# A fused two-layer gated cross-attention kernel: where ScalarE's evictions, the copy of the column sums, the normalising of x and the tail's second scores stand in the order of work

## The chip, the cores and the metric

The kernel runs on one core of one Trainium2 chip. The metric is the device time of one execution in microseconds (us), lower is better. Engines are called by their names and, in rows, by the letters of the profile: PE is TensorE (PEld its weight loads), DVE is VectorE, ACT is ScalarE, POOL is GpSimd, SP is the engine that issues DMAs here.

## The reference, cut to what matters

Batch 8, 512 tokens, width 256, 16 heads of 16, in float32. `x` and `ctx` are (8, 512, 256).

```
x = x + tanh(g_xattn[0]) * L0_xattn(layernorm(x), ctx)     # pruned softmax attention
x = x + tanh(g_ffn[0])   * L0_ffn(layernorm(x))            # fp4-rounded SwiGLU, inner width 704
x = x + tanh(g_xattn[1]) * L1_xattn(ctx, layernorm(x))     # linear attention, layer norm
x = x + tanh(g_ffn[1])   * L1_ffn(layernorm(x))            # int8-rounded linear

def L0_xattn(q, kv):                     # after the projections, per batch and head
    p    = softmax(q @ k.T / 4)          # 512 x 512
    idx  = top_k(p.sum(over queries), 460)
    p    = p * mask(idx)                 # 52 key columns are dropped, no renormalising
    return concat(p @ v) @ Wo.T + bo
```

The column sums of `p` decide which keys are dropped, so the kernel computes the scores twice: once to get row maxima, row sums and column sums, and once, much later, to make the final `p` that multiplies `v`.

## The kernel before, in words

**Units and steps.** The attention is cut into 16 units (8 batches x 2 groups of 8 heads). A unit has 16 steps; one step `z` handles two heads (h = 0, 1) and one block of 128 tokens. So the attention has 256 steps (`ALL_Z`) and a tail of 48 more (`LAST = ALL_Z + LAG + 6`, `LAG = 42`), in which only the second half of the work is left. Each engine has its own program, a loop over `z`, and the engines meet only by semaphores.

**What a step does on each engine.** TensorE at step z: two *first scores* into half of `ps_a` (L1253, it waits for the first exponentials of step z-2), two *second scores* of step z-43 into `ps_b` (it waits for the second exponentials of step z-44), two column sums into `ps_s` (L1289), two products with `v` (L1303, rows 64 to 127 of the same bank `ps_s`), and then, in most steps, a piece of a *fill*. VectorE: row maxima `nmax` (L1329) of the first scores, reciprocals (L1340), one step of the selection of the dropped keys (`rank_step`), one step of the shifts. ScalarE: the two *first exponentials* `ea` (L1428), and the *second exponentials* `prob` of step z-42 (L1444, one instruction of 1024 columns; from step 256 on two of 512 columns with a semaphore each, L1441).

**The selection.** Once per unit, at step 16u+20, VectorE copies the column sums out of `ps_s` into `rank` (`rank_step(u, 0)`, L1372). TensorE's column sums of the next unit go to the same rows and wait for that copy (`s_rank`). Seven rounds of MAX8 and MATCH_REPLACE8 follow, one instruction a step.

**Fills.** The projections of the following batches, 16 pieces of work a batch (XT0, XT1: transposes of x; CT0, CT1: of ctx; Q0, Q1, K0, K1: projections; V0, V1; GRAM; and X1, RB, KV, MM, ROW: products for the second layer), are put into the steps by a formula (`turn_of`: 0.7 pieces a step from step 41 on). TensorE issues a piece at the end of its step. Up to step 40 fills take turns in three PSUM banks; from step 41 on they have one, `ps_f`, and a fill waits until the one before it has left. A fill is moved out of PSUM by ScalarE (XT, CT, Q, K, GRAM, MM) or VectorE (the others). ScalarE does this at the end of its own step z, behind `prob`: up to step 41 for fills that end in TensorE's step z, and from step 41 on for those that end in TensorE's step z+1 (function `leaving`).

**Normalising x.** The layer norm of batch b+1 before its projections is four instructions of 128x256 in place in `x_in` (`normal`, L1011), two in ScalarE's fill GRAM of batch b and two in its fill ROW. TensorE's transposes XT0 and XT1 of batch b+1 read them. GpSimd's own in-order work there is: splitting q and k into two float16 halves (L748, L750), three small parts of a row (L738 to L742), and once a unit copying `v` into a padded tile (`pad`, L1240), which waits for TensorE.

**The tail.** From step 256 (n = z - 256) on TensorE has the last second scores and products with `v`, and beside them the first two units of the feed-forward layer: `first_product` at n = 6, 12 and 28, a transpose at 17 and 30, and `gate_or_up` (L1712, into two halves of `ps_a` in turn, moved out by ScalarE at L1887) at n = 19 to 26 and 32 to 39. In ScalarE's step the second exponentials come first, and then, where there is one, the eviction L1887.

```
            b = within(z - LAG - 1, ALL_Z)      # TensorE, step z
            if b is not None:
                second(b)
```

Of the kernel before, what the change touches and what calls it, by code (L numbers as in the profile page):

```python
# [206 lines left out]
def prepare(m, a, w, ey, tiles, bank):  # L207
# [6 lines left out]
    s_gate, s_turned = m.sem("gate"), m.sem("w_turned")  # L214
    s_w8q, s_w8t, s_bcol = m.sem("w8_rounded"), m.sem("w8_turned"), m.sem("bias_turned")
    names = {WQ: "L0_xattn_Wq", WK: "L0_xattn_Wk", WV: "L0_xattn_Wv", WO: "L0_xattn_Wo", WK1: "L1_xattn_Wk",
# [62 lines left out]
    def tensor(e):  # L279
# [13 lines left out]
        def bias_columns():  # L293
            e.wait_ge(ey.s_bias, 1)
            for n in range(2):
                for c in range(DC):
                    ins = e.transpose(bank[3][:, n * DC + c:n * DC + c + 1],
                                      brow2[:, n, c * P:c * P + P], w.ident[0:1, 0:1])
            ins.then_inc(s_bcol, 1)

# [14 lines left out]
    def scalar(e):  # L315
# [4 lines left out]
        def leave(n):  # L320
            k = TURNS.index(n)
            e.wait_ge(s_turned, k + 1)
            if n == WO:
# [12 lines left out]
        def done():  # L336

            e.wait_ge(s_turned, 6)
            e.wait_ge(s_w8t, 1)
            e.wait_ge(s_bcol, 1)  # L340

        return gate, leave, done

    def vector(e):
# [10 lines left out]
        def bias_columns():  # L355
            e.wait_ge(s_bcol, 1)
            e.tensor_scalar(ey.cols[:, 0], bank[3][:, 0:DC], 0.25, None, ALU.mult)
            e.tensor_copy(ey.cols[:, 1], bank[3][:, DC:2 * DC]).then_inc(ey.s_bias, 1)
# [215 lines left out]
def project(m, a, w, ey, scr, bank, fp4):  # L574
# [11 lines left out]
    for n in range(FILLS, FILLS * B + ROW + 1):  # L586
# [24 lines left out]
        m.sem(f"dve_{n}") for n in ("x1", "rb", "kv", "mean", "row", "c1w"))  # L611
    s_act_m, s_act_gram, s_pool_r = m.sem("act_m"), m.sem("act_gram"), m.sem("pool_r")

# [115 lines left out]
    def gpsimd(e):  # L729
# [14 lines left out]
        def halves(dst, x, c, b, stored, done):  # L744
# [5 lines left out]
            e.tensor_tensor(dst[:, 1, c], x, dst[:, 0, c], ALU.subtract).then_inc(done, 1)  # L750

        def fill(s):
            n = SEQ[s]
            if n < 0 or not real(n):
                return
            b, k = n // FILLS, n % FILLS
            if n in QK:
                e.wait_ge(s_act_full, QK.index(n) + 1)
# [10 lines left out]
    def tensor(e):  # L769
# [5 lines left out]
        def fill(s, part):  # L775
# [62 lines left out]
            elif k in (XT0, XT1):  # L838
                e.wait_ge(s_act_xn, b + 1)
                transposes(dst, ey.x_in[p], k - XT0).then_inc(s_pe_xT, 1)  # L840
# [158 lines left out]
    def scalar(e):  # L999
# [24 lines left out]
        def fill(s):  # L1024
# [48 lines left out]
            elif 0 < b < B - 1:  # L1073
                if k == Q0:
                    guess(b + 1)
                elif k in (GRAM, ROW):
                    normal(b + 1, int(k == ROW))

# [14 lines left out]
def attend(m, w, scr, tiles, fp4):  # L1093
# [156 lines left out]
    def tensor(e):  # L1250
# [55 lines left out]
        def step(z):  # L1306
            if z < ALL_Z:
                first(z)
            b = within(z - LAG - 1, ALL_Z)
            if b is not None:  # L1310
                second(b)
            g = within((z - 4) // 2, ALL_G)
# [8 lines left out]
    def vector(e):  # L1321
# [76 lines left out]
        def step(z):  # L1398
            if (z - LAG - 12) % (2 * TT) == 0:
                n = within((z - LAG - 12) // (2 * TT), 2 * UNITS)  # L1400
                if n is not None:
                    leave(n)
            if z < ALL_Z:
                maxima(z)
            if z % 2:
                g = within((z - 3) // 2, ALL_G)
                if g is not None:
                    reciprocals(g)
            u, n = (z - HALVES - 4) // HALVES, (z - HALVES - 4) % HALVES
            if 0 <= u < UNITS and n < 2 * ROUNDS + 2:  # L1410
                rank_step(u, n)
# [6 lines left out]
    def scalar(e):  # L1418
# [27 lines left out]
        def step(z):  # L1446
# [4 lines left out]
            if z < ALL_Z:  # L1451
                first(2 * z)
                first(2 * z + 1)
            b = within(z - LAG, ALL_Z)
            if b is not None:
                second(b)

        return step

# [784 lines left out]
def run(nc, whole, w, pr, fp4, pj, at, fd):  # L2244
# [5 lines left out]
    with ExitStack() as ctx:  # L2250
# [5 lines left out]

        def leaving(z):

            return [*(ended(z) if z <= pj.open else ()), *(ended(z + 1) if z >= pj.open else ())]

        @block.sync
# [114 lines left out]
        def _(e):  # L2376
            (gate, leave_weight, prepared), fill = pr.scalar(e), pj.scalar(e)
            gate()
            step = at.scalar(e)

# [26 lines left out]
            for z in range(at.last):  # L2407
                step(z)
                for s in leaving(z):
                    fill_and_magnitude(s)  # L2410
                n = z - tail
                if n == 11:
# [137 lines left out]
```

## Time and profile before

| | us |
|---|---|
| median of 3 runs | 1252.24 (1250.3 to 1255.97) |
| profiled execution: its own time | 1255.39 |
| its span, first to last instruction | 1253.7 |
| steps 0 to 40 (44.5 to 170.2) | 125.7 |
| steps 41 to 255 (170.2 to 756.4) | 586.2 |
| tail, to the last product with `v` (756.4 to 863.6) | 107.2 |
| the feed-forward and second layer (863.6 to the end) | 390.1 |

A row of the profile gives an engine, a line of the kernel, what is written and read, how many, and the times; idle time stands with the engine and line that ended it. Times in the rows are us from the start of the span, unless marked ns. The stretches of the table are bounded by starts of L1428 and the end of the last L1303.

### The profile page before, as it was taken

To read this page: it belongs to the slowest core of one execution; us is meant where nothing else is said; L and a number is where in the kernel's file an instruction comes from. 1 tells how busy PE (TensorE), PEld (TensorE's weight loads), DVE (VectorE), ACT (ScalarE), POOL (GpSimd) and SP (SyncE) were. 2 spreads that over 40 slices of the span, in tenths; PEclk is the share of its full clock that TensorE was granted. 3 is DMA by queue.
4 is the path that set the end of the run, shared out by engine and by line. 5 is a ranking of instruction groups with operands and counts; after the bars stand their busy time and mean duration, and the time that the engine had idled before them with its cause. 6 is when DMAs were issued, how large, how long until landed. Compare 5 with 4: busy or idle time off the path is not lost.

```text
span 1253.7 us, 18028 instructions
## 1 busy us (share of the span) xinstructions
PE 1102.6 (88%) x5672; PEld 493.0 (39%) x5672; DVE 1004.8 (80%) x1977; ACT 944.4 (75%) x2135; POOL 236.0 (19%) x281
## 2 busy tenths in 40 slices
PE   7898898889898888889987879888999999999974
PEld 5433332222222222222321112224667677777652
DVE  7888877787787887787889886355899999999965
ACT  5566678889888898898979996465666776766744
POOL 5433320010011011101010101101222222222212
PEclk9999998999899999999989999989999999999986
DMA  9603141232123122213202211001011111110001
GB/s 289 167 34 88 58 110 31 48 93 55 50 68 71 52 58 66 60 30 94 46 25 51 44 50 41 18 5 42 27 51 43 35 59 43 35 60 26 18 17 34
DMA packets 75986, 71.79 MB, mean 57 GB/s; under 512 B 11834, under 2 KB 69492, under 8 KB 75892
## 3 DMA queue, kind: packets, MB, share of 16 engines
q1 hardware_dynamic: 75892, 70.64, 20.8%
q8 instruction: 46, 0.75, 0.2%
q14 instruction: 48, 0.39, 0.1%
HBM read 42.83 MB, written 27.28 MB: 56 GB/s over the span
## 4 chain that ended last, share of the span: by engine, by line
PE 58%; ACT 18%; DVE 14%; issue 7%; SPq 1%; POOL 1%; DMA 1%; DVEq 0%; ACTq 0%; POOLq 0%
PE ps_s L1289 12%; PE ps_a L1712 11%; ACT ea L1428 8%; PE ps_b L1670 6%; ACT prob L1444 6%; PE ps_b L1253 4%; DVE nmax L1329 3%; PE ps_s L1303 3%; PE ps_a L1253 3%; PE ps_s L1670 2%; PE ps_f L805 2%; PE ps_f L1685 2%; PE ps_f L834 2%; PE ps_a L1721 2%; PE ps_f L1746 1%
## 5 line engine op out<-in xcount | busy, mean ns | idle before, releaser
L1428 ACT ACTIVATE ea<-ps_a,nmax 128x512 f32<-128x512 f32 x512 | 356.2, 723 | 50.4 <-DVE nmax L1329 50.0
L1329 DVE TENSOR_REDUCE nmax<-ps_a 128x2 f32<-128x1024 f32 x256 | 312.5, 1221 | 98.9 <-PE ps_a L1253 97.4
L1289 PE MATMUL ps_s<-ea,rz 128*32 128x512 f32 x1024 | 283.1, 632 | 32.4 <-DVE rank L1372 30.1
L1303 PE MATMUL ps_s<-prob,v_pad 128*32 128x512 f32 x1024 | 282.3, 632 | 2.8 <-DVE att L1396 2.4
L1444 ACT ACTIVATE prob<-ps_b 128x1024 f32<-128x1024 f32 x214 | 228.3, 1067 | 21.8 <-PE ps_b L1253 21.2
L1712 PE MATMUL ps_a<-wgu,xT 128*128 128x352 f32 x512 | 166.2, 465 | 11.8 <-ACT ea L1887 9.2
L1253 PE MATMUL ps_b<-q_st,k_st 52*128 52x512 f16 x512 | 106.3, 395 | 42.4 <-ACT prob L1444 39.2
L1428 ACT ACTIVATION_READ_ACCUMULATOR ea<-ps_a,nmax 128x1 f32 x512 | 123.5, 241 | 0.0
L1253 PE MATMUL ps_a<-k_st,q_st 48*128 48x512 f16 x512 | 102.3, 395 | 20.5 <-ACT ea L1428 19.3
L1712 PEld LDWEIGHTS ps_a<-wgu,xT 128*128 128x128 f32 x512 | 92.8, 191 | 68.4 <-issue 24.3
L1887 ACT ACTIVATE ea<-ps_a 128x352 f32<-128x352 f32 x128 | 59.7, 467 | 58.0 <-PE ps_a L1712 57.5
L1670 PE MATMUL ps_b<-wdn,hT 128*128 128x256 f32 (+1 forms) x384 | 94.9, 392 | 0.0
L1253 PEld LDWEIGHTS ps_a<-k_st,q_st 48*128 48x128 f16 x512 | 24.9, 93 | 174.9 <-ACT ea L1428 100.7
L1289 PEld LDWEIGHTS ps_s<-ea,rz 128*32 128x32 f32 x1024 | 38.0, 109 | 117.2 <-issue 112.9
L1441 ACT ACTIVATE prob<-ps_b 128x512 f32<-128x512 f32 x84 | 45.7, 596 | 43.6 <-PE ps_b L1253 43.4
L1670 PEld LDWEIGHTS ps_b<-wdn,hT 128*128 128x128 f32 (+1 forms) x384 | 67.6, 189 | 22.5 <-issue 15.9
L1383 DVE MATCH_REPLACE8 rank<-top,rank 64x512 f32<-64x512 f32 x112 | 74.9, 668 | 0.1
L1377 DVE MAX8 top<-rank 64x8 f32<-64x512 f32 x112 | 73.5, 657 | 0.1
L1253 PEld LDWEIGHTS ps_b<-q_st,k_st 52*128 52x128 f16 x512 | 26.5, 94 | 102.6 <-ACT prob L1444 62.4
L2114 DVE SCALAR_TENSOR_TENSOR ea<-ea 128x512 f32<-128x512 f32 (+1 forms) x32 | 36.0, 1126 | 18.4 <-ACT ea L1866 10.3
L1303 PEld LDWEIGHTS ps_s<-prob,v_pad 128*32 128x32 f32 x1024 | 38.4, 109 | 25.8 <-issue 24.6
L1613 POOL TENSOR_TENSOR x_in<-x_in,rows 128x512 f32<-128x512 f32 x16 | 20.4, 1274 | 127.5 <-DVE r L2051 105.6
(276 smaller groups left out, 1773.1 us busy)
## 6 DMA issues: line engine op xcount, KB each, us to landing
k_scr<-k_p SPq DMA_DIRECT2D x24, 256.0 KB, 2.5
q_scr<-q_p SPq DMA_DIRECT2D x24, 256.0 KB, 2.9
q_st<-q_scr SPq DMA_DIRECT2D x32, 192.0 KB, 4.7
k_st<-k_scr SPq DMA_DIRECT2D x32, 192.0 KB, 5.0
c_in<-in_ctx SPq DMA_DIRECT2D x8, 512.0 KB, 4.2
x_in<-in_x SPq DMA_DIRECT2D x8, 512.0 KB, 5.2
v_scr<-v_s SPq DMA_DIRECT2D x8, 512.0 KB, 4.2
v_in<-v_scr SPq DMA_DIRECT2D x16, 256.0 KB, 3.2
```

What stands on the lines that cost most here:

```text
L1253: return e.matmul(bank, left[b][o:o + rows, r, t * P:t * P + P], right[b][o:o + rows, r], start=True, stop=True)
L1289: e.matmul(ps_s[32 * h:32 * h + 32, :], rz[:, t, r, 2 * k + h, o:o + 32], ea[g % RING][:, 2 * k + h], start=(n == 0 and k == 0), stop=(n = ...
L1303: e.matmul(ps_s[o:o + 32, :], v_pad[u % 2][:, t, 4 * r + 2 * k + h], at.prob[g % PROBS][:, 2 * k + h], start=(t == 0 and k == 0), stop=(t ...
L1329: e.tensor_reduce(nmax[u % 2][:, t].rearrange("p (h r) -> p r h", h=2)[:, r], ps_a[:, z % 2 * 2:z % 2 * 2 + 2], AX_X, ALU.max, negate=True ...
L1377: e.max(top[:, :], rank[:, :]).then_inc(*dv.up())
L1383: e.match_replace(rank[:, :], top[:, :], rank[:, :], NEG).then_inc(*dv.up())
L1428: e.activation(ea[c % RING][:, g % 4], ps_a[:, g % 4], ACT.Exp, bias=nmax[u % 2][:, t, n:n + 1], accum_out=tot[u % 2][:, t, n:n + 1]).then ...
L1441: e.activation(dst[:, h], ps_b[:, h], ACT.Exp).then_inc(done, 1)
L1444: e.activation(dst, ps_b[:, :, :], ACT.Exp).then_inc(s_prob, 1)
L1670: ins = e.matmul(dst[t], left(c, t), right(c), start=(first and c == chunks[0]), stop=(last and (apart or t == N - 1) and c == chunks[-1]))
L1712: ins = e.matmul(gu[:, q % 2, 0:HALF_F], xT[:, c, t * P:t * P + P], w.wgu[:, c, k * HALF_F:(k + 1) * HALF_F], start=(c == 0), stop=(c == D ...
L1887: e.activation(dst[:, t, k % 2 * HALF_F:(k % 2 + 1) * HALF_F], gu[:, q % 2, 0:HALF_F], func).then_inc(s_act_gu, 1)
```

## The change

Five edits. (1) ScalarE: the second exponentials become a function of their own (`later`), and fills that end in TensorE's step z leave in ScalarE's step z, between the first and the second exponentials. (2) VectorE: `rank_step(u, 0)`, the copy of the column sums, stands ahead of the step's maxima. (3) `normal` of batches 2 to 7 moves from ScalarE to GpSimd, at the same two fills; the transposes of these batches wait for a new semaphore of GpSimd. (4) TensorE, from step 256 on: second scores of step z-42 (at step 256 those of z-43 too). (5) One semaphore of the preparation is merged into another, which leaves its waits where they were.

```diff
@@ TensorE's fill: XT0, XT1
-                e.wait_ge(s_act_xn, b + 1)
+                if b < 2:
+                    e.wait_ge(s_act_xn, b + 1)
+                else:
+                    e.wait_ge(s_pool_xn, b - 1)
@@ GpSimd's fill
+        def normal(b, half):
+            p = b % 2
+            e.wait_ge(s_dve_nb, b + 1)
+            for t in (2 * half, 2 * half + 1):
+                ins = e.tensor_scalar(ey.x_in[p][:, t], ey.x_in[p][:, t], rs[p][:, t:t + 1], nb[p][:, t:t + 1],
+                                      ALU.mult, ALU.add)
+            if half:
+                ins.then_inc(s_pool_xn, 1)
...
+            if 0 < b < B - 1 and k in (GRAM, ROW):
+                normal(b + 1, int(k == ROW))
@@ ScalarE's fill
-                elif k in (GRAM, ROW):
-                    normal(b + 1, int(k == ROW))
@@ TensorE's step
-            b = within(z - LAG - 1, ALL_Z)
-            if b is not None:
-                second(b)
+            if z <= ALL_Z:
+                b = within(z - LAG - 1, ALL_Z)
+                if b is not None:
+                    second(b)
+            if z >= ALL_Z:
+                b = within(z - LAG, ALL_Z)
+                if b is not None:
+                    second(b)
@@ VectorE's step
+            u, n = (z - HALVES - 4) // HALVES, (z - HALVES - 4) % HALVES
+            if 0 <= u < UNITS and n == 0:
+                rank_step(u, n)
             if z < ALL_Z:
                 maxima(z)
...
-            if 0 <= u < UNITS and n < 2 * ROUNDS + 2:
+            if 0 <= u < UNITS and 0 < n < 2 * ROUNDS + 2:
                 rank_step(u, n)
@@ ScalarE's step and loop
             if z < ALL_Z:
                 first(2 * z)
                 first(2 * z + 1)
+
+        def later(z):
             b = within(z - LAG, ALL_Z)
...
                 step(z)
-                for s in leaving(z):
+                for s in ended(z):
                     fill_and_magnitude(s)
+                later(z)
```

ScalarE, steps around the evictions of two projections, with `ea` the first exponentials, `prob` the second and `full` the eviction of a fill. Before:

```order
L1428 ACTIVATE ea,tot0<-ps_a,nmax0 128x512 x2
L1444 ACTIVATE prob1<-ps_b 128x1024
L1022 ACTIVATE full1<-ps_f,cols 128x512
L1428 ACTIVATE ea,tot0<-ps_a,nmax0 128x512 x2
L1444 ACTIVATE prob1<-ps_b 128x1024
```

and after:

```order
L1446 ACTIVATE ea,tot0<-ps_a,nmax0 128x512 x2
L1035 ACTIVATE full1<-ps_f,cols 128x512
L1462 ACTIVATE prob1<-ps_b 128x1024
L1446 ACTIVATE ea,tot0<-ps_a,nmax0 128x512 x2
L1462 ACTIVATE prob2<-ps_b 128x1024
```

The eviction `full1` stands one pair of first exponentials later in ScalarE's program, and the second exponentials that were ahead of it are behind it.

VectorE, the step in which the column sums are copied (`rank<-ps_s`). Before:

```order
L881 BN_STATS st0<-x_in0 128x6 x2
L1329 TENSOR_REDUCE nmax0<-ps_a 128x2
L1372 TENSOR_SCALAR rank<-ps_s 64x512
L1363 STREAM_TRANSPOSE row1<-part 128x128
L1329 TENSOR_REDUCE nmax0<-ps_a 128x2
```

and after:

```order
L894 BN_STATS st0<-x_in0 128x6 x2
L1388 TENSOR_SCALAR rank<-ps_s 64x512
L1345 TENSOR_REDUCE nmax0<-ps_a 128x2
L1379 STREAM_TRANSPOSE row1<-part 128x128
L1345 TENSOR_REDUCE nmax0<-ps_a 128x2
```

One row of maxima and the copy changed places; nothing else on this engine moves.

TensorE, steps 255 to 257, with `ps_b` the second scores and `ps_s` the column sums and products with `v`. Before:

```order
L1253 MATMUL ps_b<-q_st1,k_st1 128x512 x2
L1289 MATMUL ps_s<-ea,rz 32x512 x2
L1303 MATMUL ps_s<-prob2,v_pad1 32x512 x2
L1253 MATMUL ps_b<-q_st1,k_st1 128x512 x2
L1289 MATMUL ps_s<-ea,rz 32x512 x2
L1303 MATMUL ps_s<-prob0,v_pad1 32x512 x2
```

and after:

```order
L1264 MATMUL ps_b<-q_st1,k_st1 128x512 x2
L1300 MATMUL ps_s<-ea,rz 32x512 x2
L1314 MATMUL ps_s<-prob2,v_pad1 32x512 x2
L1264 MATMUL ps_b<-q_st1,k_st1 128x512 x4
L1300 MATMUL ps_s<-ea,rz 32x512 x2
L1314 MATMUL ps_s<-prob0,v_pad1 32x512 x2
```

Two second scores were added at step 256, so that every later step of the tail issues those of one step further on.

## Rows read from the trace of the kernel before

**Rows 1.** The page: busy us (share of the span) and instructions by engine.
```profile
PE 1102.6 (88%) x5672; PEld 493.0 (39%) x5672; DVE 1004.8 (80%) x1977; ACT 944.4 (75%) x2135; POOL 236.0 (19%) x281
```
**Rows 2.** Windows: length, busy time and count by engine, PEclk, DMA share, GB/s.
```profile
44.50:170.24 125.74, 112.52 (x474) 44.74 (x472) 104.92 (x196) 82.85 (x219) 48.17 (x57) 0.95 0.30 83
170.24:636.00 465.76, 409.83 (x2427) 120.97 (x2425) 368.68 (x702) 416.81 (x917) 50.04 (x81) 0.97 0.24 60
```
**Rows 3.** ScalarE's groups, 170.24 to 756.4: busy us, mean ns, idle before, releasers.
```profile
L1428 ACT ACTIVATE ea<-ps_a,nmax 128x512 f32<-128x512 f32 x430 | 300.4, 729 | 11.9 <-DVE nmax L1329 11.7
L1444 ACT ACTIVATE prob<-ps_b 128x1024 f32<-128x1024 f32 x214 | 228.3, 1067 | 21.8 <-PE ps_b L1253 21.2
...
L1022 ACT ACTIVATE full<-ps_f,cols 128x512 f32<-128x512 f32 x16 | 11.0, 688 | 10.7 <-PE ps_f L864 6.0 <-PE ps_f L819 4.8
L1011 ACT ACTIVATE x_in<-x_in,nb,rs 128x256 f32<-128x256 f32 x16 | 8.7, 602 | 0.0
L1059 ACT ACTIVATE m_s<-ps_f,m_mean 128x256 f32<-128x256 f32 x12 | 5.0, 471 | 6.9 <-DVE m_mean L978 6.9
...
L1044 ACT ACTIVATE gram<-ps_f 128x512 f32<-128x512 f32 x5 | 3.0, 598 | 2.9 <-PE ps_f L805 2.9
```
**Rows 4.** Timeline, ScalarE, around one half of `normal`.
```profile
505.42 1.09 ACT L1011 ACTIVATE x_in<-x_in,nb,rs 128x256 f32<-128x256 f32 x2
506.41 0.68 ACT L1428 ACTIVATE ea<-ps_a,nmax 128x512 f32<-128x512 f32 x1
```
**Rows 5.** Timeline, step 147: start, us, engine, line, idle before.
```profile
472.27 0.62 PE L1289 MATMUL ps_s<-ea,rz 128*32 128x512 f32 x2 [1.95 <-DVE rank L1372]
...
473.27 1.12 PE L819 MATMUL ps_f<-cT,wt 128*128 128x512 f32 x2
...
474.43 0.69 ACT L1022 ACTIVATE full<-ps_f,cols 128x512 f32<-128x512 f32 x1 [2.30 <-PE ps_f L819]
...
475.86 1.13 PE L819 MATMUL ps_f<-cT,wt 128*128 128x512 f32 x2
```
**Rows 6.** Timeline, VectorE, the step of one copy of the column sums.
```profile
336.30 1.21 DVE L1329 TENSOR_REDUCE nmax<-ps_a 128x2 f32<-128x1024 f32 x1
337.42 0.67 DVE L1372 TENSOR_SCALAR rank<-ps_s 64x512 f32<-64x512 f32 x1
```
**Rows 7.** TensorE's longest waits, 170.24 to 756.4: us, times, longest.
```profile
PE ps_b L1253 <- ACT prob L1444: 39.2, 77, 0.9
PE ps_s L1289 <- DVE rank L1372: 24.2, 13, 2.7
...
PE ps_f L805 <- ACT m_s L1059: 1.2, 3, 0.7
```
**Rows 8.** Windows before and behind the wait of rows 6 (columns of rows 2).
```profile
334.00:338.30 4.30, 1.12 (x12) 0.38 (x13) 4.23 (x10) 4.30 (x11) 0.00 (x0) 1.00 0.01 2
338.30:341.70 3.40, 3.40 (x16) 0.45 (x20) 1.08 (x2) 1.46 (x5) 0.00 (x0) 0.50 0.03 3
```
**Rows 9.** Timeline, one step of the tail with `gate_or_up`.
```profile
800.08 1.42 PE L1712 MATMUL ps_a<-wgu,xT 128*128 128x352 f32 x4 [0.64 <-ACT ea L1887]
...
801.75 1.05 PE L1303 MATMUL ps_s<-prob,v_pad 128*32 128x512 f32 x4
801.92 1.09 ACT L1441 ACTIVATE prob<-ps_b 128x512 f32<-128x512 f32 x2 [1.98 <-PE ps_b L1253]
```
**Rows 10.** TensorE's waits, 756.4 to 863.6: us, times, longest.
```profile
PE ps_a L1712 <- ACT ea L1887: 8.0, 12, 0.7
```
**Rows 11.** GpSimd's groups with 256 columns: busy us, mean ns, idle before, releasers.
```profile
L1240 POOL COPY v_pad<-v_in 128x256 f32<-128x256 f32 x32 | 11.8, 398 | 170.6 <-PE ps_s L1303 170.6
L740 POOL TENSOR_TENSOR r_s<-r_s,r_p 1x256 f32<-1x256 f32 x16 | 10.6, 661 | 1.3
```
**Rows 12.** Timeline, a small VectorE instruction beside one of GpSimd.
```profile
788.45 1.27 POOL L1613 TENSOR_TENSOR x_in<-x_in,rows 128x512 f32<-128x512 f32 x1
...
788.60 1.14 DVE L2058 TENSOR_TENSOR tm<-tm,ve_b 128x4 f32<-128x4 f32 x1
```

More of the change, by code:

```diff
@@ L214, in prepare @@
     s_gate, s_turned = m.sem("gate"), m.sem("w_turned")
-    s_w8q, s_w8t, s_bcol = m.sem("w8_rounded"), m.sem("w8_turned"), m.sem("bias_turned")
+    s_w8q, s_w8t = m.sem("w8_rounded"), m.sem("w8_turned")
     names = {WQ: "L0_xattn_Wq", WK: "L0_xattn_Wk", WV: "L0_xattn_Wv", WO: "L0_xattn_Wo", WK1: "L1_xattn_Wk",
@@ L298, in bias_columns @@
                                       brow2[:, n, c * P:c * P + P], w.ident[0:1, 0:1])
-            ins.then_inc(s_bcol, 1)
+            ins.then_inc(s_turned, 1)
         def turn_w8():
@@ L321, in leave @@
             k = TURNS.index(n)
-            e.wait_ge(s_turned, k + 1)
+            e.wait_ge(s_turned, k + 1 + (k >= TURNS.index(WQ)))
             if n == WO:
@@ L336, in done @@
         def done():
-            e.wait_ge(s_turned, 6)
+            e.wait_ge(s_turned, 7)
             e.wait_ge(s_w8t, 1)
-            e.wait_ge(s_bcol, 1)
         return gate, leave, done
@@ L355, in bias_columns @@
         def bias_columns():
-            e.wait_ge(s_bcol, 1)
+            e.wait_ge(s_turned, 3)
             e.tensor_scalar(ey.cols[:, 0], bank[3][:, 0:DC], 0.25, None, ALU.mult)
@@ L611, in project @@
         m.sem(f"dve_{n}") for n in ("x1", "rb", "kv", "mean", "row", "c1w"))
-    s_act_m, s_act_gram, s_pool_r = m.sem("act_m"), m.sem("act_gram"), m.sem("pool_r")
+    s_act_m, s_act_gram, s_pool_r, s_pool_xn = (m.sem(n) for n in ("act_m", "act_gram", "pool_r", "pool_xn"))
     s_pe_xT, s_pe_cT, s_pe_q, s_pe_k, s_pe_v = (m.sem(f"pe_{n}") for n in ("xT", "cT", "q", "k", "v"))
@@ L1408, in step @@
                     reciprocals(g)
-            u, n = (z - HALVES - 4) // HALVES, (z - HALVES - 4) % HALVES
-            if 0 <= u < UNITS and n < 2 * ROUNDS + 2:
+            if 0 <= u < UNITS and 0 < n < 2 * ROUNDS + 2:
                 rank_step(u, n)
@@ L1456, in step @@
                 second(b)
-        return step
+        return step, later
     at.sync, at.gpsimd, at.tensor, at.vector, at.scalar = sync, gpsimd, tensor, vector, scalar
@@ L2255, in ended @@
             return pj.ends_at.get(z, ())
-        def leaving(z):
-            return [*(ended(z) if z <= pj.open else ()), *(ended(z + 1) if z >= pj.open else ())]
         @block.sync
@@ L2378, in _ @@
             gate()
-            step = at.scalar(e)
+            step, later = at.scalar(e)
             def fill_and_magnitude(s):
```

## The prediction

> **What bounds the kernel now.** I read the page first: no engine is full over the span, TensorE 88%, VectorE 80%, ScalarE 75% [rows 1]. That average hides stages, so I cut the span at the starts of the first exponentials. In steps 41 to 180 or so (the stretch 170 to 636) ScalarE is busy 416.8 of 465.8 us, TensorE 409.8, VectorE 368.7; in steps 0 to 40 ScalarE is busy 82.9 of 125.7 and VectorE 104.9 [rows 2]. The five edits act on the first two thirds and on the tail; behind 863.6 us nothing is moved, and those 390 us I take as they are.
>
> In the stretch 170.24 to 756.4 (586.2 us, 215 steps) a step without a fill costs ScalarE two first exponentials of 729 ns and one second of 1067 ns, some 2.3 us with their ends overlapping. It idles where a row says so: in front of the second exponentials 21.2 us for TensorE's scores, in front of the first 11.7 us for the maxima, and in front of evicted fills 10.7 (projections) + 6.9 (MM) + 2.9 (GRAM), with some 2.6 in smaller groups: 23.1 us [rows 3]. All of this, some 57 us, is time of the stage, since ScalarE does nothing but run through its list in order. TensorE is second: it waits 39.2 us for second exponentials (room that ScalarE's pace leaves it), and 24.2 us, 13 times, for the copy of the column sums [rows 7].
>
> **The terms.** All are taken from the profiled execution, 1255.4 us, which is 3.2 above the median of the runs (1252.2).
>
> *Normalising on GpSimd.* ScalarE loses 24 instructions, 16 of them in this stretch, of 602 ns each [rows 3]. A pair takes the engine 0.99 us (505.42 to 506.41) [rows 4], so 8 pairs give 7.9 us. The 4 pairs in steps 0 to 40 I put at nothing: there the next first exponentials wait for VectorE or TensorE anyway. What GpSimd pays is not in the trace. Its nearest rows are a one-input copy of 256 columns, 0.40 us, and a two-input operation of 256 columns, 0.66 us [rows 11]; one tensor input makes me take 0.45, 1.8 us a batch, between 1.6 and 2.6. It is covered: both halves need only the statistics, ready at fill K0, so GpSimd can do them as soon as its last half of k is split, and the transposes that wait follow some 7 steps (over 15 us) later. Queued behind it are only the row parts, which wait on VectorE longer than that, and a `pad`, which waits for TensorE. Without the cover it would be 1.8 us of TensorE a batch, 11 us.
>
> On the choice of engine the Trainium skill speaks against this edit: "GPSIMD Engine Reference", section 4.1, gives elementwise work to VectorE and calls GpSimd about half as fast for two inputs and roughly level for one; our rows agree with the second half, 0.40 us for one input against 0.66 for two. By its per-element figure (section 3.1) 256 columns would be 0.22 us and a dispatch, an estimate near the lower row. That would leave the sum as it is, because the price is hidden.
>
> *Evictions between the exponentials.* Step 147 shows the old order: `prob` has ended at 472.13 (474.43 less the idle of 2.30), TensorE issues the last piece of the fill at 473.27, and ScalarE stands 2.30 us until it can evict at 474.43, with the next first exponentials (their maxima long ready or soon to be) behind it [rows 5]. In the new order the fill of TensorE's step z leaves behind the first exponentials of step z, two times 729 ns, 1.4 us, of work later, and ahead of a `prob` whose scores TensorE issues after that fill. The normal wait of one eviction is some 0.3 to 1 us and is covered by those 1.4 us. I take 20 of the 23.1 us; the ends are 0 (the same arrival is then waited for at `prob`) and 23.1.
>
> *Column sums copied first.* Of the 2 us of such a wait 1.12 us is the maxima that stand ahead of the copy (336.30 to 337.42) [rows 6]. What they delay is TensorE's column sums, and all that is behind these: the products, the fill, the next first scores. Behind the wait the clock is also lower: at 338.3 the granted clock falls from 1.00 to 0.50, from 2.4 to 1.2 GHz, for 3.4 us in which TensorE is busy throughout, after a stretch of 4.3 us with only 1.12 busy [rows 8]. Cost: the maxima and the first exponentials of that step come 0.67 us later, mostly inside room, since ScalarE is still at `prob`. 13 times 1.12 is 14.6 us, plus a part of the lower clock (up to 1.7 us each, 13 times, as 3.4 us at half clock do the work of 1.7), less the cases where ScalarE had not idled: I take 14 us here and 2 x 1.2 = 2.4 us for the two in steps 0 to 40. Ends: 8 and 30.
>
> *Tail.* A step with `gate_or_up` runs: gate at 800.08, products at 801.75, which last 1.05 us, then TensorE waits 0.6 to 0.7 us for L1887, which stands in ScalarE's list behind a `prob` that started only at 801.92 [rows 9]. With the second scores one step ahead, ScalarE has done that `prob` and the eviction before TensorE gets there. The wait is 8.0 us in 12 steps [rows 10], all on TensorE, which is busy for the rest of these steps. At step 256 TensorE does two pairs of second scores with a `prob` between them, once, about 1 us. Term: 7. Ends: 0 and 9.
>
> *The merged semaphore* leaves the waits as they were: 0.
>
> *What is given back.* TensorE and VectorE come nearer to being the bound. One known place: with one bank, the next fill can't start before the eviction ends. Now the next piece comes 0.74 us after it (475.12 to 475.86) [rows 5], and this interval, or one under 0.9 us, is found at 22 of 49 evictions; the eviction now comes up to 1.4 us later in ScalarE's order, so perhaps 0.2 to 0.4 us of TensorE for these 22: 5 us.
>
> Sum: 7.9 + 20 + 14 + 2.4 + 7 - 5 = 46.3. 1255.4 - 46.3 = 1209.1, and against the median 1252.2 - 46.3 = 1206.
>
> **The rivals.**
> *The next engine takes it* (0.2). ScalarE's floor in 170 to 636 is its 416.8 busy less 8 us; TensorE was busy 409.8 [rows 2], a difference that a few bursts of fills use up. For: rows 7, where TensorE waits for ScalarE briefly and often, so it is never far ahead. Against: its 39.2 us of waits for `prob` are room. If half of the 34 us of evictions and copies comes back as waits for maxima or scores: 1206 + 17 = 1223.
> *More than the sum* (0.12). If the copy's wait and the lower clock behind it vanish in nearly all units: the second term goes from 14 to 28 us, the wait for the bank to nothing: 1206 - 19 = 1187.
> *The evictions' wait only changes its name* (0.06). `prob` waits instead, as long as before: 1206 + 20 = 1226, and with the bank's wait doubled, 1231.
> *GpSimd and VectorE in each other's way* (0.04). A VectorE instruction of only 128x4 took 1.14 us beside a GpSimd one of 1.27 [rows 12]. If each of the 24 new instructions stopped VectorE for its whole 0.45 to 0.66 us, and VectorE were late in each case: 11 to 16 us, 1217 to 1222. The same page of the Trainium skill ("GPSIMD Engine Reference", section 1) says that the two share their SBUF interfaces when VectorE runs a 2-port mode or two SBUF inputs; the trace agrees in rows 12, two SBUF inputs. Against it as a loss: the maxima and the copy of the sums read PSUM.
> *Slower: the single bank* (0.03). If the eviction, in its new place, holds `ps_f` by the whole pair of exponentials, 1.4 us, at each of 49 evictions, and TensorE is what everything waits for, that is 69 us lost, the eviction term is gone and the other terms stay but for TensorE's 5: 1252 - 31 + 69 = 1290. The case turns at 31/49 = 0.6 us an eviction. For: the 22 intervals under 0.9 us. Against: TensorE now waits only 1.2 us in all for a fill evicted by ScalarE [rows 7], and it has up to 0.7 us of interval before it loses any.
> *No measurable change* (0.03): gains and the bank's wait cancel, 1252.
>
> **How the numbers follow.** The likeliest (0.52) is 1206, with 1196 to 1216 as its own range from the ends of its terms that can't all fall together. For 8 in 10 I reach up to the next-engine case and part of the renamed wait, 1226, and down to 1190, most of the way to the larger gain. 0.5% of 1252 is 6 us, about what a measurement of this kernel can tell from no change. Faster by more than that: all but the last two, 0.94; within it 0.03; slower 0.03.
>
> **What would show it.** In the profile after: 16 fewer ScalarE instructions of 128x256 in the stretch from step 41 to 255, and that stretch down from 586 to about 542 us; L1022, L1044 and L1059 of before with idle of 3 us or less together; the wait of the column sums for `rank` down from 2 us a time to under 1; the copy ahead of the maxima; fewer windows at half clock; in the tail no wait of `gate_or_up` for its evictions and 107 us down to 100; TensorE never waiting for GpSimd's x. Wrong, if ScalarE's idle in front of `prob` grows by what the evictions lose, if TensorE's waits for a fill's bank sum to over 10 us, or if VectorE's late maxima take over.

## The result

| | before, us | after, us |
|---|---|---|
| median | 1251.72 (4 runs, 1250.3 to 1255.97) | 1189.91 (4 runs, 1188.59 to 1190.23) |
| ratio | | 0.9499 (0.9475 to 0.9523) |
| span of the profiled execution | 1253.7 | 1186.9 |
| steps 0 to 40 | 125.7 | 120.6 |
| steps 41 to 255 | 586.2 | 537.3 |
| tail | 107.2 | 96.0 |
| the rest | 390.1 | 388.8 |
| stretches of TensorE at half clock, steps 0 to 255 | 17 | 2 |

The changed kernel is 61.8 us (5.0%) faster. The forecast was 46, to 1206, and 1190 as the low end of its range; the time lies just beneath that end. The profiled execution of before was 3.7 us above its median, that of after 1.3 below, so the two spans differ by 66.8 us and not by 61.8. (Steps 41 to 255 end with the last second exponentials of 1024 columns: at 702.1 us here; in the kernel before at 755.9, 0.5 us sooner than the bound that its table uses.)

The page after, busy us and instructions by engine, and the clock by slices:

```profile
PE 1074.5 (91%) x5672; PEld 488.6 (41%) x5672; DVE 1004.1 (85%) x1977; ACT 928.1 (78%) x2111; POOL 249.9 (21%) x305
...
PEclk9999999999999999999999999999999999999995
```

Against [rows 1], GpSimd has 24 instructions and 13.9 us more, ScalarE 24 instructions and 16.3 us less. TensorE has as many instructions as before and is busy 28.1 us less: the same matmuls at a higher clock (over the whole span it stood at half clock for 96 us before and 41 after, and half of the difference is 27.6). The windows after, for steps 0 to 40, 41 to 211, 212 to 255, and the tail (columns as in [rows 2]):

```profile
44.10:164.70 120.60, 109.61 (x475) 43.84 (x474) 105.51 (x196) 78.83 (x210) 53.53 (x65) 0.97 0.31 87
164.70:602.60 437.90, 405.07 (x2507) 122.29 (x2507) 381.25 (x732) 418.59 (x928) 60.37 (x101) 1.00 0.26 64
602.60:702.00 99.40, 74.97 (x520) 15.28 (x518) 87.97 (x155) 99.30 (x223) 9.04 (x21) 1.00 0.20 47
702.00:798.00 96.00, 92.82 (x381) 28.66 (x381) 49.92 (x117) 64.28 (x119) 8.27 (x9) 0.98 0.08 22
```

In the third row ScalarE is busy 99.30 of 99.40 us: that stage is now at ScalarE's floor. From step 41 to 255 the clock is 1.00 throughout, where it was 0.96 before. (The stretch 170 to 636 of [rows 2], with 0.97, ends in step 207. The prediction called it steps 41 to 180.) ScalarE's groups in the same stretch, to be held against [rows 3]:

```profile
L1446 ACT ACTIVATE ea<-ps_a,nmax 128x512 f32<-128x512 f32 x430 | 315.1, 798 | 15.1 <-DVE nmax L1345 14.7
L1462 ACT ACTIVATE prob<-ps_b 128x1024 f32<-128x1024 f32 x214 | 243.5, 1138 | 2.3 <-PE ps_b L1264 1.7
...
L1035 ACT ACTIVATE full<-ps_f,cols 128x512 f32<-128x512 f32 x16 | 11.7, 729 | 0.0
...
L1072 ACT ACTIVATE m_s<-ps_f,m_mean 128x256 f32<-128x256 f32 x12 | 5.0, 470 | 2.2 <-DVE m_mean L991 2.1
...
L1057 ACT ACTIVATE gram<-ps_f 128x512 f32<-128x512 f32 x5 | 3.1, 614 | 0.0
```

Read the last column. The idle before evictions is 2.2 us, where it was 23.1; before `prob` it is 2.3, where it was 21.8. Only the wait for the maxima stays, 15.1 against 11.9. (The first two groups' mean durations are longer than before, 798 against 729 and 1138 against 1067 ns, while all of ScalarE's busy time in steps 41 to 255 fell from 529.3 to 517.9 us. Where one instruction follows directly on the other, the two records overlap: the pair of first exponentials starts 0.66 us apart in both kernels. So the busy time of the window is the one to compare.) TensorE's waits in this stretch, against [rows 7]:

```profile
PE ps_b L1264 <- ACT prob L1462: 36.9, 69, 1.3
PE ps_s L1300 <- DVE rank L1388: 10.1, 9, 1.7
...
PE ps_f L782 <- ACT cT L1052: 1.6, 3, 0.5
PE ps_f L815 <- ACT m_s L1072: 1.4, 3, 0.6
```

The wait for the copy of the column sums went from 24.2 us in 13 waits to 10.1 in 9. One such copy, in the timeline of after:

```profile
314.25 0.66 DVE L1388 TENSOR_SCALAR rank<-ps_s 64x512 f32<-64x512 f32 x1
...
314.94 1.23 DVE L1345 TENSOR_REDUCE nmax<-ps_a 128x2 f32<-128x1024 f32 x1
...
315.06 0.62 PE L1300 MATMUL ps_s<-ea,rz 128*32 128x512 f32 x2 [1.52 <-DVE rank L1388]
```

The copy ends at 314.91 and TensorE goes on at 315.06, with the maxima now beside it and not ahead of it. A matmul pair takes 0.62 us, full clock.

### The profile page after: what moved, and what is told of

Its sections match the earlier page's. It is cut to its first block, busy times and chain, and to the rows that moved or that the text cites. A ratio compares the mean times of both kernels' runs of the same rounds, so it can differ in the third digit from the quotient of the medians.

```text
span 1186.9 us, 18040 instructions
## 1 busy us (share of the span) xinstructions
PE 1074.5 (91%) x5672; PEld 488.6 (41%) x5672; DVE 1004.1 (85%) x1977; ACT 928.1 (78%) x2111; POOL 249.9 (21%) x305
## 4 chain that ended last, share of the span: by engine, by line
PE 52%; ACT 22%; DVE 16%; issue 7%; SPq 1%; POOL 1%; DMA 1%; ACTq 0%; DVEq 0%; POOLq 0%
PE ps_a L1732 11%; ACT ea L1446 10%; ACT prob L1462 8%; PE ps_s L1300 8%; PE ps_b L1690 7%; DVE nmax L1345 4%; PE ps_s L1314 4%; PE ps_b L1264 2%; PE ps_s L1690 2%; PE ps_a L1264 2%; PE ps_f L1705 2%; PE ps_a L1741 2%; PE ps_f L815 2%; PE ps_f L1766 1%; PE ps_f L844 1%
## 5 line engine op out<-in xcount | busy, mean ns | idle before, releaser
L1446 ACT ACTIVATE ea<-ps_a,nmax 128x512 f32<-128x512 f32 x512 | 370.8, 781 | 53.7 <-DVE nmax L1345 53.3
L1300 PE MATMUL ps_s<-ea,rz 128*32 128x512 f32 x1024 | 271.9, 609 | 16.0 <-DVE rank L1388 13.7
L1314 PE MATMUL ps_s<-prob,v_pad 128*32 128x512 f32 x1024 | 269.5, 606 | 2.9 <-DVE att L1412 2.5
L1462 ACT ACTIVATE prob<-ps_b 128x1024 f32<-128x1024 f32 x214 | 243.5, 1138 | 2.3 <-PE ps_b L1264 1.7
L1446 ACT ACTIVATION_READ_ACCUMULATOR ea<-ps_a,nmax 128x1 f32 x512 | 149.5, 299 | 0.0
L1264 PE MATMUL ps_b<-q_st,k_st 52*128 52x512 f16 x512 | 103.0, 384 | 40.7 <-ACT prob L1462 38.7
L1732 PEld LDWEIGHTS ps_a<-wgu,xT 128*128 128x128 f32 x512 | 92.3, 190 | 58.0 <-issue 14.6
L1459 ACT ACTIVATE prob<-ps_b 128x512 f32<-128x512 f32 x84 | 45.6, 597 | 31.3 <-PE ps_b L1264 31.3
```

Of the source, the lines that this page charges most:

```text
L1264: return e.matmul(bank, left[b][o:o + rows, r, t * P:t * P + P], right[b][o:o + rows, r], start=True, stop=True)
L1300: e.matmul(ps_s[32 * h:32 * h + 32, :], rz[:, t, r, 2 * k + h, o:o + 32], ea[g % RING][:, 2 * k + h], start=(n == 0 and k == 0), stop=(n = ...
L1314: e.matmul(ps_s[o:o + 32, :], v_pad[u % 2][:, t, 4 * r + 2 * k + h], at.prob[g % PROBS][:, 2 * k + h], start=(t == 0 and k == 0), stop=(t ...
L1446: e.activation(ea[c % RING][:, g % 4], ps_a[:, g % 4], ACT.Exp, bias=nmax[u % 2][:, t, n:n + 1], accum_out=tot[u % 2][:, t, n:n + 1]).then ...
L1459: e.activation(dst[:, h], ps_b[:, h], ACT.Exp).then_inc(done, 1)
L1462: e.activation(dst, ps_b[:, :, :], ACT.Exp).then_inc(s_prob, 1)
```

## The experiments

**Two theories.** A: the terms are right and separate, and the surplus is spread over them. B: the surplus is in one term, the copy of the column sums, because the wait also sets the clock of what follows it and all of that reaches ScalarE. The first eight kernels take out one edit of the changed kernel ("no") or make one alone in the kernel before ("only"); the four after them take the copy's cost apart. All times are medians. The kernels ran in three groups (the "no" kernels, the "only" kernels, the last four), each with its own executions of the kernel before, to which the ratios are (its medians: 1251.82, 1252.73 and 1252.60). The changed kernel's own kernel before had 1251.72, so a difference between groups can be off by a microsecond from this alone. "Theory 1" and "theory 2" in the expectations are A and B.

**no_evict.** Fills leave behind `prob` again, one step later for fills from step 41 on.

```diff
+        def leaving(z):
+            return [*(ended(z) if z <= pj.open else ()), *(ended(z + 1) if z >= pj.open else ())]
...
-                for s in ended(z):
-                    fill_and_magnitude(s)
                 later(z)
+                for s in leaving(z):
+                    fill_and_magnitude(s)
```

> The changed kernel with the evictions of fills back behind the second exponentials. Theory 1 (the terms of the sum were right in kind, and each is its own): the 20 us term comes back, 1190 + 20 = 1210, with ScalarE's idle in front of evicted fills back to some 20 us in steps 41 to 255 and no stretch at half clock beyond those of the changed kernel. Theory 2 (TensorE's clock is a term of its own that the sum left out, fed by the gaps on TensorE): late fills leave TensorE no longer gaps than now, so the clock stays up, and also 1210. Rival (the evictions only took over waits that the other edits would have taken): less than 1200.

1206.24 us, ratio 0.9631 (0.9593 to 0.9669): 16.3 us slower than the changed kernel, where 20 was expected. ScalarE's idle time in front of evicted fills is back, 19.4 us in steps 41 to 255:

```profile
ACT m_s L1072 <- DVE m_mean L991: 6.8, 6, 2.0
ACT full L1035 <- PE ps_f L877: 4.0, 8, 0.9
ACT full L1035 <- PE ps_f L829: 3.6, 8, 1.2
ACT gram L1057 <- PE ps_f L815: 2.9, 5, 1.3
ACT xT L1066 <- PE ps_f L782: 1.4, 2, 1.2
```

(and 0.7 for cT). But both theories said that no further stretch at half clock would come, and two did in steps 41 to 255, beside one more than the changed kernel has in steps 0 to 40. TensorE stood at half clock for 24.8 us up to step 255, against 6.8 in the changed kernel.

**no_rank.** The copy stands behind the maxima again.

```diff
-            u, n = (z - HALVES - 4) // HALVES, (z - HALVES - 4) % HALVES
-            if 0 <= u < UNITS and n == 0:
-                rank_step(u, n)
             if z < ALL_Z:
...
-            if 0 <= u < UNITS and 0 < n < 2 * ROUNDS + 2:
+            u, n = (z - HALVES - 4) // HALVES, (z - HALVES - 4) % HALVES
+            if 0 <= u < UNITS and n < 2 * ROUNDS + 2:
                 rank_step(u, n)
```

> The changed kernel with the copy of the column sums behind the maxima again. Theory 1: 14 + 2.4 us come back, 1206, that is 1.1 us a copy and little else. Theory 2 (the clock): TensorE's longer wait, some 2 us a unit, brings most of the stretches at half clock back (the kernel before had 17 up to the end of the attention, the changed one 2), and 25 us or more come back, 1215 or above.

1221.65 us, 0.9760 (0.9721 to 0.9799): 31.7 us slower, twice the term of 16.4. This speaks for B. Its stretch of steps 41 to 255 is 560.4 us against 537.3, with 8 stretches at half clock against none (the last of them reaches into the tail).

**no_norm.** Batches 2 to 7 are normalised by ScalarE again.

```diff
-            if 0 < b < B - 1 and k in (GRAM, ROW):
-                normal(b + 1, int(k == ROW))
...
-                if b < 2:
-                    e.wait_ge(s_act_xn, b + 1)
-                else:
-                    e.wait_ge(s_pool_xn, b - 1)
+                e.wait_ge(s_act_xn, b + 1)
...
+                elif k in (GRAM, ROW):
+                    normal(b + 1, int(k == ROW))
```

> The changed kernel with x normalised by ScalarE again. Theory 1: 8 us, 1198, all of it in steps 41 to 180, where ScalarE is now busy nearly all the time. Theory 2: the same. Rival (GpSimd's instructions cost VectorE as much as they relieve ScalarE, or VectorE and TensorE bound the stretch now): within 3 us of 1190.

1198.45 us, 0.9574 (0.9537 to 0.9612): 8.5 us slower, against a term of 7.9. Of the profiled executions steps 41 to 255 take 545.3 us, 8.0 more than in the changed kernel.

**no_tail.** TensorE's second scores are those of step z-43 in the tail too.

```diff
-            if z <= ALL_Z:
-                b = within(z - LAG - 1, ALL_Z)
-                if b is not None:
-                    second(b)
-            if z >= ALL_Z:
-                b = within(z - LAG, ALL_Z)
-                if b is not None:
-                    second(b)
+            b = within(z - LAG - 1, ALL_Z)
+            if b is not None:
+                second(b)
```

> The changed kernel with the tail's second scores one step later again, as before. Theory 1: 7 us, 1197. Theory 2 (the tail's stretch shrank by 11.2 us, from 107.2 to 96.0, and all of it is this edit): 11 us, 1201, with the waits of gate_or_up for its evictions 8 us of them and the rest in the waits of second scores around ScalarE's silu.

1200.08 us, 0.9581 (0.9541 to 0.9620): 10.2 us slower, against 7; theory 2 had said 11. TensorE's waits in its tail:

```profile
PE ps_a L1727 <- ACT ea L1902: 8.0, 12, 0.7
PE ps_b L1264 <- ACT prob L1454: 2.3, 1, 2.3
PE ps_a L1707 <- DVE xg L2138: 1.3, 1, 1.3
PE ps_b L1264 <- ACT prob L1457: 0.9, 1, 0.9
```

and in the tail of the changed kernel:

```profile
PE ps_b L1264 <- ACT prob L1462: 1.9, 1, 1.9
PE ps_b L1264 <- ACT prob L1459: 1.4, 1, 1.4
PE ps_s L1314 <- DVE att L1412: 0.9, 2, 0.6
PE ps_a L1712 <- DVE xg L2143: 0.6, 1, 0.6
```

The 8.0 us of [rows 10] are gone as a whole. The change's own price, the `prob` between two pairs of second scores, is in the second list, and both lists have such waits for `prob`: 3.2 us without the edit and 3.3 with it.

**only_evict, only_rank, only_norm, only_tail.** One edit each in the kernel before: the diffs of the four kernels above, with + and - exchanged. All four hold the merged semaphore, and so do all the kernels made from the changed one: what it does by itself was not measured.

> The kernel before with only the evictions moved between the exponentials. Theory 1: 20 us of 1252, 1232. Theory 2 (clock): the waits for the copy of the column sums and the half clock behind them stay, so ScalarE waits at prob what it does not wait at evictions near them, and 15 to 20 us are gained, 1232 to 1237, with 10 or more stretches at half clock left up to the end of the attention.

1234.63 us, 0.9865 (0.9837 to 0.9893): 18.1 us faster than before, within theory 2's times. 9 stretches at half clock are left in steps 0 to 255, one fewer than it said.

> The kernel before with only the copy of the column sums ahead of the maxima. Theory 1: 14 + 2.4 us, 1236. Theory 2 (clock): half or more of the 17 stretches at half clock vanish and 20 to 25 us are gained, 1227 to 1232.

1230.48 us, 0.9829 (0.9807 to 0.9850): 22.3 us faster, as theory 2 said, and 7 of the 17 stretches at half clock are left.

> The kernel before with only the normalising on GpSimd. Theory 1: 8 us, 1244. Rival (ScalarE then waits for the fill or the scores instead): under 4 us, 1248 or more.

1246.11 us, 0.9951 (0.9934 to 0.9969): 6.6 us faster, between the two. Steps 41 to 255 of the profiled executions are 8.0 us shorter than in the kernel before.

> The kernel before with only the tail's second scores one step earlier. Theory 1: 7 us, 1245. Theory 2: 11 us, 1241, the stretch from the last first exponential to the last product with v 96 us as in the changed kernel.

1241.88 us, 0.9918 (0.9892 to 0.9944): 10.9 us faster, as theory 2 said; its tail takes 97.3 us, where 96 was said.

The four gains add up to 57.8 us by medians; the four losses of the "no" kernels add up to 66.8; the whole is 61.8. Three edits are worth about the same alone as last in (evictions 18.1 and 16.3, normalising 6.6 and 8.5, tail 10.9 and 10.2). The copy is worth 22.3 alone and 31.7 last in. Theory A, separate terms with a spread surplus, fails there.

**busy_wait.** no_rank, and in 13 of its waits for the copy TensorE multiplies columns of zeros by `prob`, adding them to `ps_s`. This adds work whose products are zero, takes nothing out, and leaves the copy as late as in no_rank.

```diff
+            if n == 0 and k == 0 and u >= 3:
+                gv = g - LAG // 2
+                e.wait_ge(s_prob, 2 * gv + 1)
+                for _ in range(2):
+                    for h in range(2):
+                        e.matmul(ps_s[SUMS + 32 * h:SUMS + 32 * h + 31, :], rz[:, t, r, h, FIRST_ROW + 1:FIRST_ROW + 32],
+                                 at.prob[gv % PROBS][:, h], start=False, stop=False)
```

> The changed kernel with the copy behind the maxima again (no_rank, 1221.7 us), and in 13 of the 15 waits for the copy TensorE multiplies zero weights by prob, two pairs of 128x512 products, about 1.8 us, added to the accumulating values: the results stay the same, the copy is as late as in no_rank, but TensorE isn't idle. If the lower clock behind the gap is half of the 31.8 us: most of the 8 half-clock stretches in steps 41 to 255 vanish and 1205 to 1212. If the late copy itself is what costs (the clock a symptom): 1220 or more, as the extra products are no shorter than some of the waits.

1208.75 us, 0.9650 (0.9624 to 0.9675): 12.9 us faster than no_rank, by useless work. Windows of no_rank, before and behind one wait for the copy (columns as in [rows 2]):

```profile
238.50:240.50 2.00, 0.04 (x2) 0.00 (x0) 1.97 (x4) 2.00 (x6) 0.32 (x1) 1.00 0.01 4
240.50:243.90 3.40, 2.96 (x10) 0.73 (x10) 0.60 (x2) 1.19 (x4) 0.00 (x0) 0.51 0.02 2
```

and of busy_wait, at the same copy:

```profile
238.50:240.50 2.00, 1.94 (x10) 0.47 (x10) 1.97 (x3) 2.00 (x6) 0.73 (x1) 1.00 0.01 4
240.50:243.90 3.40, 2.93 (x20) 0.62 (x21) 1.15 (x4) 1.60 (x5) 0.00 (x0) 1.00 0.02 2
```

The first busy column is TensorE's. In no_rank it stands for two us, the granted clock behind that is 0.51, and 2.96 us of work hold 10 matmuls. In busy_wait it has 1.94 us of work in the same two us, the clock stays at 1.00, and 2.93 us hold 20. The same copy in TensorE's timeline of no_rank:

```profile
240.94 1.07 PE L1300 MATMUL ps_s<-ea,rz 128*32 128x512 f32 x2 [2.40 <-DVE rank L1388]
```

and in that of busy_wait:

```profile
238.88 1.91 PE L1301 MATMUL ps_s<-prob,rz 128*31 128x512 f32 x8
241.26 0.62 PE L1307 MATMUL ps_s<-ea,rz 128*32 128x512 f32 x2 [0.47 <-DVE rank L1395]
```

The same pair of column sums takes 1.07 us at half clock and 0.62 at full. In steps 41 to 255 the stretches at half clock go from 8 to 1 (the one that reaches into the tail) and the time from 560.4 to 551.2 us. So 9.2 us are seen where the extra products stand. The two profiled executions differ by 10.4 us and the medians, which come from two groups, by 12.9: the clock's part in these 13 waits is 9 to 13 us.

**no_rank_sums_last.** no_rank, and in the step of a copy TensorE issues its column sums behind the products with `v` and the fill, so that real work stands in the wait.

```diff
-            if g is not None:
+            if g is not None and not put_off(z):
                 column_sums(g, z % 2)
...
+        def put_off(z):
+            return z > HALVES and z % HALVES == 4
+
+        def late_sums(z):
+            g = within((z - 4) // 2, ALL_G)
+            if g is not None and put_off(z):
+                column_sums(g, z % 2)
...
                     fill(s, part)
+                late_sums(z)
```

> The copy behind the maxima again, but in these steps TensorE does its products with v and its piece of a fill first and the column sums last, so that real work lies in the wait. If the gap on TensorE and the clock behind it are the cost: 1195 to 1203, nearly all of the 31.8 us back with a copy as late as before. If the copy must come early for the first exponentials of the later steps: above 1210.

1194.04 us, 0.9535 (0.9506 to 0.9564), just under the 1195 to 1203 expected: 27.6 of the 31.7 us are back, with the copy as late as before. No stretch at half clock is left in steps 0 to 255. TensorE's waits for the copy, in no_rank and here:

```profile
PE ps_s L1300 <- DVE rank L1388: 32.3, 15, 3.2
PE ps_s L1300 <- DVE rank L1396: 9.5, 9, 1.7
```

and the windows of steps 0 to 40 and 41 to 255, two of no_rank and then two of this kernel:

```profile
45.20:169.40 124.20, 111.38 (x474) 44.23 (x472) 104.77 (x196) 78.95 (x210) 54.26 (x66) 0.95 0.30 82
169.40:729.80 560.40, 490.44 (x3023) 139.04 (x3021) 469.73 (x886) 520.25 (x1151) 69.63 (x121) 0.98 0.23 59
43.80:159.80 116.00, 106.59 (x475) 43.49 (x475) 105.00 (x196) 78.50 (x211) 53.36 (x65) 1.00 0.32 88
159.80:705.10 545.30, 493.72 (x3023) 139.20 (x3021) 469.37 (x886) 519.62 (x1151) 69.35 (x121) 1.00 0.25 61
```

Steps 41 to 255 win back 15.1 us, of the 23.1 by which no_rank is longer there than the changed kernel. Another 8.2 come from steps 0 to 40, where this kernel, with 116.0 us, is faster than the changed one with 120.6. So a late copy still costs some 8 us in steps 41 to 255.

**after_sums_last.** The same reordering in the changed kernel, so it differs from no_rank_sums_last in the place of the copy alone.

> The changed kernel with the column sums last in the step of the copy too. 13.7 us of waits for the copy are left on TensorE; ScalarE has 17 us of idle left in steps 41 to 255. If they are connected, 2 to 5 us, 1185 to 1188; if ScalarE's remaining waits have other causes, 1190.

1185.15 us, 0.9466 (0.9440 to 0.9493), the lowest time measured. TensorE's waits for the copy in steps 0 to 255 fall from 13.7 us to 1.3. It is 4.8 us below the changed kernel by medians, but the two ratios' intervals overlap, and the two profiled executions differ by 0.9 us only (spans of 1186.0 and 1186.9). What it adds to the changed kernel is small, and zero is not ruled out. Against no_rank_sums_last, in the same group, it is 8.9 us faster, 7.7 of them in steps 41 to 255 (537.6 against 545.3 us), both at a clock of 1.00 there: this is what the copy's place is worth when the clock no longer falls.

**after_copy_step_end.** The copy stands at the end of VectorE's step before, behind that step's maxima and ahead of the next.

```diff
-            u, n = (z - HALVES - 4) // HALVES, (z - HALVES - 4) % HALVES
-            if 0 <= u < UNITS and n == 0:
-                rank_step(u, n)
             if z < ALL_Z:
...
+            u, n = (z - HALVES - 3) // HALVES, (z - HALVES - 3) % HALVES
+            if 0 <= u < UNITS and n == 0:
+                rank_step(u, n)
```

> The changed kernel with the copy moved further ahead, to the end of VectorE's step before, in front of its fill work. VectorE then waits for the column sums of that step, up to 1 us a unit, and the remaining 13.7 us of TensorE's waits vanish. If TensorE's wait is still on the path: 1185 to 1188. If VectorE's own wait makes its fills and maxima later by as much: 1190 to 1193.

1188.42 us, 0.9492 (0.9466 to 0.9518), between the two expected times and the same as the changed kernel within the noise. TensorE's waits for the copy did not vanish, as had been expected:

```profile
PE ps_s L1300 <- DVE rank L1388: 9.7, 11, 2.1
```

against 13.7 us in 11 waits. So this place gains nothing that shows; whether a copy that removed the wait would gain more was not tried here.

**How much of it is the clock.** Every execution has its mean granted clock, and executions of one kernel differ in it. Over the executions of the kernel before in the three groups (11, 17 and 9), clocks from 0.955 to 0.968 went with times from 1261 to 1245 us: 0.73 to 1.00 us for each 0.001 of clock, by a straight line through each group. Mean clocks by kernel:

| kernel | executions | mean clock | median us |
|---|---|---|---|
| before | 37 | 0.961 to 0.962 | 1251.8 to 1252.7 |
| only_rank | 4 | 0.9695 | 1230.5 |
| no_rank | 6 | 0.9640 | 1221.7 |
| busy_wait | 5 | 0.9770 | 1208.8 |
| changed kernel | 4 | 0.9808 | 1189.9 |
| no_evict | 6 | 0.9757 | 1206.2 |
| no_norm | 6 | 0.9772 | 1198.5 |
| no_tail | 6 | 0.9807 | 1200.1 |

From no_rank to busy_wait it is 0.0130 of clock and 12.9 us, 0.99 us for each 0.001, at the upper end of those slopes. The last edit in, from no_rank to the changed kernel, brings 0.0168, worth 12 to 17 us; the same edit alone, from before to only_rank, 0.0084, worth 6 to 8. Most of the difference between 31.7 and 22.3 is this, by these slopes. The half-clock time of the profiled executions up to step 255 agrees: the edit takes it from 58 to 38 us alone and from 39.5 to 6.8 last in, and half of that is 10 and 16 us. The whole change brings 0.019, 14 to 19 us of the 61.8. The other edits have a share in it: the clock of no_evict is 0.0051 below the changed kernel's, worth 4 to 5 of its 16.3 us, and that of no_norm 0.0036, 3 to 4 of its 8.5; no_tail's is the same as the changed kernel's.

## Why the prediction was right and where it was wrong

The sum came to 46.3 us and 61.8 were measured. Of the 15.5 us between them the copy of the column sums is the largest part, 5.9 (measured alone) to 15.3 (last in); the tail is 3 to 4; the 5 us taken off as given back do not show as a loss; the evictions, forecast too large, take 2 to 4 off again. The edits act on each other, so these do not add up exactly.

**The bound and the direction: right.** ScalarE's idle time in steps 41 to 255 was taken to be the stage's time. It fell from 56.9 to 19.4 us (537.3 less 517.90), ScalarE's work fell by 11.4, and the stage by 48.9.

**Normalising on GpSimd: right.** 7.9 forecast, 6.6 alone and 8.5 last in. In steps 41 to 255, which the term was worked out for, it is 8.0 both times. What GpSimd pays is a middle duration of 556 ns, between the two rows that bounded it (0.40 and 0.66), though above the 0.45 taken:

```profile
L755 POOL TENSOR_SCALAR x_in<-x_in,rs,nb 128x256 f32<-128x256 f32 x24 | 14.2, 605 | 0.0
```

The mean is pulled up by three longer ones, 740, 856 and 1247 ns. Hidden it stays: no wait of TensorE for `s_pool_xn` shows. Nor did VectorE suffer, as one rival feared: it is busy 469.2 us in steps 41 to 255, against 469.8 before. The estimate from the Trainium skill ("GPSIMD Engine Reference", section 3.1), 0.22 us and a dispatch, lies further below the 556 ns, and would have been equally harmless. The two rows that the prediction set beside section 4.1 compare one input with two on GpSimd, and not GpSimd with VectorE, so they neither bear that section out nor speak against it.

**Evictions between the exponentials: right in kind, too large.** 20 forecast, 16.3 to 18.1 measured, and by the mean clocks 4 to 5 us of the 16.3 are clock, which the term did not count. The idle that it named is gone, 23.1 to 2.2 us. Some 3 us came back as later maxima (11.9 to 15.1), which is the rival "the next engine takes it" at a fifth of its size.

**Column sums copied first: the step that failed.** The mechanism stood in the prediction with both its parts, 1.12 us of maxima and up to 1.7 us of lower clock, for 15 copies. Then it took off "the cases where ScalarE had not idled", and came to 14 us, plus 2.4 in steps 0 to 40: 16.4. The maxima alone are 14.6 us there, so the discount swallowed the whole of the clock's part, however large that was taken, and 0.6 us more. It had no row behind it. Measured: 22.3 alone, 31.7 last in.

Without a discount the two parts explain this. In steps 41 to 255 no_rank is 23.1 us longer than the changed kernel; 13 times 1.12 is 14.6, and the clock, measured apart by busy_wait, is 9.2 there (0.7 a copy, or 1.0 by medians, where up to 1.7 was said): together 23.8. ScalarE's idle time in the three steps from a copy on, over the 13 copies, shows that all of it arrives there: 31.3 us in no_rank, 22.1 in busy_wait, 7.1 in the changed kernel. That is 9.2 less by the clock and 15.0 less by the copy's place, 1.9 a copy in all. What the change alone brings is less, because with the old evictions the clock falls again elsewhere: only_rank has 10 stretches at half clock before the tail's start less than before, but still 7.

The rival "more than the sum" named this: the copy's wait and the clock behind it vanish, 1187. It had 0.12. By its own time it was 3 us off.

**Tail: mis-sized.** 7 forecast, 10.2 to 10.9 measured. The 8.0 us of waits for L1887 went as a whole, and not 7 of them. The step at 256 had been charged 1 us; but waits for `prob` stand in the tail with and without the edit alike (3.3 and 3.2 us), so it cost nothing net, and `xg` is waited for 0.7 us less. The remaining 1.5 to 2.2 us were not traced.

**What is given back: mis-placed.** TensorE's waits for `ps_f` to leave by ScalarE did grow, from [rows 7]'s 1.2 us to 5.8 (1.6 + 1.4 + 0.7 + 0.7, and 1.4 in smaller groups), by 4.6 us, as large as the 5 forecast. But they cost the kernel nothing that shows: TensorE still has 36.9 us of waits for `prob`, so they come out of its room, and ScalarE's idle before `prob` fell to 2.3 us. The price was right and was set against the wrong account. This is read from the waits; no kernel was run that takes this price out alone. The rival of the single bank turned at 0.6 us for each of 49 evictions; 5.8 us in all is 0.12 each, which refutes it.

**What would show it.** 16 ScalarE instructions of 128x256 gone (`normal` has no row left on ScalarE there), the stretch at 537 where 542 was said, idle before evictions 2.2 where 3 was the limit, the copy ahead of the maxima, the tail at 96 where 100 was said, no wait of `gate_or_up` for its evictions: all as said. The wait for the copy was to be under 1 us a time: it is 1.1 where it still occurs, so this sign failed narrowly, and 0.8 over the 13 copies.

**Shown and only argued.** That a gap of TensorE costs clock and that this costs time is shown by busy_wait. That the copy's place costs something beside the clock is shown by the two kernels with the column sums last, 8.9 us apart with no fall of the clock in steps 41 to 255 in either. With the old order of TensorE's work it is 13.9 us there (551.2 in busy_wait less 537.3), against 7.7 with the sums last, so about half of it comes from the work that is queued behind the wait. That the interaction of 9 us is the clock's rests on mean clocks, slopes and the half-clock time of single executions; it was not tried apart, and 2 us or so of it stay open.

## What to carry to other kernels

Price a wait of TensorE at three things: its own length, the work that is queued behind it, and the lower clock of that work. Take a discount off a cost only where a row shows the idle time that would absorb it, and, the other way round, don't charge an engine that has room. If a wait can't be removed, put work into it that doesn't depend on it: moving the column sums behind the products and the fill on the waiting engine gave 27.6 us, where the earlier copy had given 31.7. And measure an edit both alone and last in: the copy was worth 22.3 and 31.7.

## What the runs showed of the hardware

TensorE's clock fell from 2.4 to 1.2 GHz (granted 1.00 to 0.5) at the end of a wait of 2.4 us in no_rank, for 3.4 us, and did not fall when the same wait was filled with matmuls of zeros: more work made the kernel 12.9 us faster by medians. The Trainium skill ("Perfetto Trace Analysis", section "Matmul Optimizations") says that matmuls should be issued back to back in batches, since the engine scales its power with its utilization; these runs agree, in a stage where TensorE was busy 490.44 of 560.40 us.

The mean granted clock of an execution goes with its time within the kernel before: 0.73 to 1.00 us for each 0.001, so executions 16 us apart were the same program at a mean clock of 0.955 and 0.968.
